# The attention output of batches 0 to 2 is turned by transfers and scaled by GpSimd

## The reference, cut to what matters

```python
def attention(Q, K, V, ...):                        # K = V = ctx
    q = _split_heads(Q @ Wq.T + bq)
    k = _split_heads(K @ Wk.T + bk)
    v = _split_heads(V @ Wv.T + bv)
    attn = softmax(einsum('bhqd,bhkd->bhqk', q, k) * scale)
    ctx = einsum('bhqk,bhkd->bhqd', attn, v)        # heads side by side: (B, S, 256)
    return ctx @ Wo.T + bo
x = x + tanh(g_xattn) * attention(layernorm(x), ctx, ctx, ...)
h = layernorm(x)
logits = h @ w_router                               # top 2 of 8, softmax over the two
moe    = sum over the two of score * ((silu(h @ fc1[e]) * gate) @ fc2[e])
shared = (silu(h @ gate_w) * (h @ up_w)) @ down_w
x = x + tanh(g_ffn) * (moe + shared)
```

## Time and profile before

| what | value |
|---|---|
| time, median of 3 runs | 473.4 us (473.13 to 475.3) |
| profiled execution | 472.9 us |
| its span | 471.2 us |
| PE busy | 461.7 us, 98% |
| DVE busy | 338.4 us, 72% |
| ACT busy | 255.7 us, 54% |
| POOL busy | 118.4 us, 25% |

### The profile page before, as it was taken

The page is one execution under the profiler, slowest core; times in us unless marked ns, Lnnn a source line. Parts: engine busy times, 40 slices in busy tenths (PEclk is TensorE's granted clock), DMA queues, the critical chain, the costliest instruction groups (busy, mean ns, idle before and its releaser), DMA issues.

```text
span 471.2 us, 8172 instructions
## 1 busy us (share of the span) xinstructions
PE 461.7 (98%) x2394; PEld 224.7 (48%) x2394; DVE 338.4 (72%) x858; ACT 255.7 (54%) x544; POOL 118.4 (25%) x143
## 2 busy tenths in 40 slices
PE   8999999999999999999999999999999999999997
PEld 8665422333333333333356564675555555555745
DVE  1888897888888888888847876665565656542574
ACT  1664476777777777777766212113676667631110
POOL 5594485000000000000001177640333223332000
PEclk9999999999999999999999999999999999999999
DMA  8668762956564555320000022232332223211931
GB/s 254 219 179 230 184 198 69 198 141 134 136 134 137 135 134 137 92 69 1 3 1 2 0 102 90 91 110 60 92 87 83 85 87 91 80 57 47 362 114 59
DMA packets 47532, 52.80 MB, mean 112 GB/s; under 512 B 8640, under 2 KB 39744, under 8 KB 47488
## 3 DMA queue, kind: packets, MB, share of 16 engines
q1 hardware_dynamic: 42688, 41.75, 33.1%
q0 software_dynamic: 3168, 8.69, 5.1%
q10 hardware_dynamic: 1632, 1.84, 1.2%
HBM read 34.52 MB, written 17.60 MB: 111 GB/s over the span
## 4 chain that ended last, share of the span: by engine, by line
PE 83%; DVE 6%; DMA 5%; SPq 3%; issue 1%; ACT 1%; POOL 1%; ACTq 0%; POOLq 0%; DVEq 0%
PE PS L1329 12%; PE PS L1241 11%; PE PS L1457 11%; PE PS L1504 10%; PE PS L1611 9%; PE PS L1517 6%; PE PS L1630 5%; PE PS L1606 3%; PE PS L1377 3%; PE PS L1292 3%; PE PS L1625 2%; PE PS L1339 2%; DMA X<-in_x_dram 2%; PE PS L1585 2%; PE PS L1593 2%; DMA q_parts<-R 1%
## 5 line engine op out<-in xcount | busy, mean ns | idle before, releaser
L782 DVE TENSOR_REDUCE nmax<-PS 128x1 f32<-128x512 f32 x256 | 161.8, 681 | 14.7 <-PE PS L1241 14.2
L664 ACT ACTIVATE R<-PS 128x512 f32<-128x512 f32 x256 | 133.2, 603 | 38.9 <-PE PS L1457 38.9
L1241 PE MATMUL PS<-R 96*128 96x512 bf16 x256 | 96.0, 381 | 0.7 <-DMA R<-k_parts 0.5
L1457 PE MATMUL PS<-R 98*128 98x512 bf16 x256 | 86.2, 379 | 1.8 <-DMA R<-mparts 1.5
L1329 PE MATMUL PS<-R 128*32 128x512 f32 x512 | 68.2, 605 | 0.0
L552 POOL DMA_INDIRECT token_y<-R,dest x34 | 32.8, 966 | 86.6 <-DVE R L1124 86.3
L1241 PEld LDWEIGHTS PS<-R 96*128 96x128 bf16 x256 | 24.8, 97 | 56.3 <-DVE nmax L782 39.4
L513 POOL TENSOR_TENSOR rstd<-var_eps,minus_half 128x4 f32<-128x4 f32 x4 | 4.1, 1024 | 187.7 <-DVE var_eps L765 187.7
L1611 PE MATMUL PS<-R 128*128 x100 | 47.3, 595 | 1.0 <-ACT R L738 1.0
L1457 PEld LDWEIGHTS PS<-R 98*128 98x128 bf16 x256 | 24.7, 97 | 41.1 <-ACT R L664 20.9
L683 ACT ACTIVATE R<-PS 128x512 f32<-128x512 f32 x16 | 9.6, 597 | 62.0 <-PE PS L1504 62.0
(11 more groups left out here) (173 smaller groups left out, 602.5 us busy)
## 6 DMA issues: line engine op xcount, KB each, us to landing
R<-q_parts SPq DMA_DIRECT2D x96, 64.0 KB, 3.1
R<-k_parts SPq DMA_DIRECT2D x96, 64.0 KB, 3.2
R<-in_fc_w_dram SPq DMA_DIRECT2D x16, 256.0 KB, 3.0
R<-token_y SPq DMA_DIRECT2D x4, 1024.0 KB, 10.2
R<-slot_x SPq DMA_DIRECT2D x25, 129.0 KB, 2.1
k_parts<-R SPq DMA_DIRECT2D x8, 384.0 KB, 3.2
q_parts<-R SPq DMA_DIRECT2D x8, 384.0 KB, 3.6
fc<-in_fc_w_dram SPq DMA_DIRECT2D x16, 128.0 KB, 3.0
```

Of the source, the lines that this page charges most:

```text
L664: nc.scalar.activation(PT[:, kt, j, :], PS[:, (G * (TB * i + kt) + j) % 3, :], ACT.Exp).then_inc(exp_done, 1)
L782: nc.vector.tensor_reduce(nmax[:, i % 2, j * TB + qt:j * TB + qt + 1], PS[:, smax_bank(n), :], AX.X, ALU.max, negate=True).then_inc(max_re ...
L1241: mm(PS[:, smax_bank(n), :], QS[g][0:KS, j, qt * P:(qt + 1) * P], KST[g][0:KS, j, :], start=True, stop=True).then_inc(smax_done, 1)
L1457: mm(PS[:, n % 3, :], KST[g][0:KM, j, kt * P:(kt + 1) * P], QS[g][0:KM, j, :], start=True, stop=True).then_inc(st_done, 1)
```

## The change

The context of the groups 0 to 11 (batches 0 to 2, `TURNED` = 12) keeps its features on partitions. SP stores the copy `OT` of a group to DRAM and sends the row of denominators of each head into `DENS`, 16 columns on 128 partitions. A group later SP reads the rows of features back, packed, as 64 partitions of `CTX` (which lies in the memory of `CH`); DVE takes the reciprocal in `DENS`' layout (`scale_of`), SP stores it, and another group later reads it back, repeated for the 16 features of each head, as 64 partitions of `SCALES` (the memory of the value weights). Once two groups are there, POOL multiplies 128x512 of `CTX` by `SCALES`. `out_projection` reads `CTX` in place. The transposes, `denominators` and `head_out` stay for batch 3.

With it: the experts' weights are loaded by POOL; the wait `parts_stored` moves from ahead of the loop into it; the tail's steps stand in another order; the column of token numbers in `CH` is written by POOL for each batch after its projection; `router_rows(3)` goes ahead of half a product; the last parts of the shared product of batch 1, their `shared_out` and the scales of the experts move into slots 0 to 2.

```diff
 @block.sync
+ def store_out(i):
+     sp.wait_ge(ot_ready, i + 1)
+     sp.dma_start(o_scr[i], OT[i % 2]).then_inc(o_out[i % 2], 16)
+     sp.dma_start(DENS[:, i % 2, :], OT[i % 2][DK:P:P // G, :].rearrange("j (q n) -> j q n", n=G * TB)).then_inc(den_in[i % 2], 16)
+ def load_out(i):
+     b, g = divmod(i, NG)
+     sp.wait_ge(o_out[i % 2], times(i))
+     sp.dma_start(CTX[64 * (g % 2):64 * (g % 2 + 1), b, g // 2, :],
+                  o_scr[i].rearrange("(j d) n -> j d n", j=G)[:, 0:DK, :]).then_inc(ctx_in[i // 2], 16)
+ def store_scale(i):
+     sp.wait_ge(scale_ready, i + 1)
+     sp.dma_start(r_scr[i].rearrange("j (q n) -> (j q) n", n=G * TB), SCALE[:, i % 2, :]).then_inc(scale_out[i % 2], 16)
+ def load_scale(i):
+     sp.wait_ge(scale_out[i % 2], times(i))
...
+     wait(sp, ctx_scaled, i // 2)
+     sp.dma_start(SCALES[64 * (i % 2):64 * (i % 2 + 1), :],
+                  r_scr[i].unsqueeze(1).to_broadcast([G, DK, S])).then_inc(ctx_in[i // 2], 16)
...
- for b in range(1, B):
-     parts_stored(b)
  for i in range(GROUPS):
+     if i and (i + 3) % NG == 0 and i + 3 < GROUPS:
+         parts_stored((i + 3) // NG)
      if 0 < i and i + 3 < GROUPS:
          load_group(i + 3)
      if i + 1 < GROUPS:
          load_max(i + 1)
...
-     if 2 <= i < 2 + E:
...                                   # 4 DMAs of fc1, fc2
+     if 0 <= i - 1 < TURNED:
+         store_out(i - 1)
+     if 0 <= i - 2 < TURNED:
+         load_out(i - 2)
+         store_scale(i - 2)
+     if 0 <= i - 3 < TURNED:
+         load_scale(i - 3)
 @block.gpsimd
  def rstd_second(b):
...
+     pool.wait_ge(wo_done, 2 * (b + 1))
+     nc.gpsimd.iota(CH[:, sl, D], ...).then_inc(tokens_in, 1)
+ def scale_context(n):
+     b, c = divmod(n, DC)
+     pool.wait_ge(ctx_in[n], 16 * 4)
+     nc.gpsimd.tensor_tensor(CTX[:, b, c, :], CTX[:, b, c, :], SCALES, ALU.mult).then_inc(ctx_scaled, 1)
...
+ for i in range(2, TURNED + 3):
+     if i < 2 + E:
+         pool.wait_ge(m2_ready, i + 2)
+         load_expert(i - 2)            # the 4 DMAs of fc1, fc2
+     if i >= 4 and i % 2 == 0:
+         scale_context((i - 4) // 2)
 @block.scalar
  def out_copy(i):
      act.wait_ge(pv_done, TB * (i + 1))
-     if i >= 2:
-         act.wait_ge(ot_t, i - 1)
+     if 2 <= i < TURNED + 2:
+         act.wait_ge(o_out[i % 2], times(i - 2))
+         act.wait_ge(den_in[i % 2], times(i - 2))
...
 @block.vector
+ def scale_of(i):
+     dve.wait_ge(den_in[i % 2], times(i))
...
+     nc.vector.reciprocal(SCALE[:, i % 2, :], DENS[:, i % 2, :]).then_inc(scale_ready, 1)
  def tail(n):
-     0: ctt_second(0)    1: residual(0), statistics(0)    2: ctt_second(1), normalised(0)
-     3: residual(1), statistics(1)    4: h2t_second(0), ctt_second(2), normalised(1)
-     5: logits_turned(0), logits(0), choose(0), residual(2), statistics(2)
+     0: residual(0), statistics(0)    2: normalised(0), residual(1), statistics(1)
+     3: h2t_second(0)    4: normalised(1), logits_turned(0), residual(2), logits(0)
+     5: statistics(2), choose(0)
  in the loop, behind the sixth maximum of group i:
+     if 0 <= i - 2 < TURNED:
+         scale_of(i - 2)
-     denominators(i - 1), head_out(i - 1) for every i
+     ... for i > TURNED
 @block.tensor
  def tail(n):
-     0: ctx_transpose(0)    1: out_projection(0)    2: ctx_transpose(1)    3: out_projection(1)
-     4: h2_transpose(0), ctx_transpose(2)
-     5: router(0), out_projection(2, (0,)), router_rows(0), out_projection(2, (1,))
+     0: out_projection(0)    1: out_projection(1, (0,))    2: out_projection(1, (1,))
+     3: h2_transpose(0), out_projection(2, (0,))
+     4: router(0), out_projection(2, (1,)), router_rows(0)
+     5: h2_transpose(1)
...
-         if kt == 1 and i:
+         if kt == 1 and i > TURNED:
              out_transpose(i - 1)
...
  values(GROUPS - 1, TB - 1)
- h2_transpose(1)
  rank(0)
...
- gate_up(1, 1)
+ gate_or_up(1, 1, 0)
  router_rows(3)
+ gate_or_up(1, 1, 1)
...
- down(BE - 1, 2)
+ down(BE - 1, TB)
  transpose_rows(0)
- down_part(BE - 1, IC - 1, 2)
- down_part(BE - 1, IC - 1, 3)
+ down_part(BE - 1, IC - 1, 0)
+ down_part(BE - 1, IC - 1, 1)      # parts 2 and 3 follow in slots 0 and 1
```

More of the change, by code:

```diff
@@ L304, in ctt, with times @@
         def ctt(b, c):
-            return CTT[:, b % 2, c, :]
+            return CTX[:, b, c, :] if b < B - 1 else CTT[:, c, :]
+        def times(i):
+            return 16 * (i // 2 + 1)
         @block.sync
@@ L1063, in _ @@
                             one_max(TB * s + qt)
-                        if i:
-                            n = TB * kt + qt - OUT_AT
-                            if n == 0:
-                                denominators(i - 1)
-                            elif n == 1:
-                                head_out(i - 1)
+                        n = TB * kt + qt - OUT_AT
+                        if n == 0 and 0 <= i - 2 < TURNED:
+                            scale_of(i - 2)
+                        if n == 0 and i > TURNED:
+                            denominators(i - 1)
+                        if n == 1 and i > TURNED:
+                            head_out(i - 1)
                         if TB * kt + qt == M2_AT and i + 1 < GROUPS:
@@ L1109, in _, with scales, slot_result @@
             tabulate_units()
-            for h in range(2):
-                shared_out(1, h)
-            dve.wait_ge(exp_sc, 1)
-            step(nc.vector.tensor_scalar(sc[:, 2, :], sc[:, 1, :], 1.0, None, ALU.add))
-            step(nc.vector.reciprocal(sc[:, 3, :], sc[:, 2, :]))
-            step(nc.vector.tensor_tensor(sc[:, 0, :], sc[:, 1, :], sc[:, 3, :], ALU.mult))
-            step(nc.vector.tensor_scalar(scg[:, 0, :], sc[:, 3, :], tg[:, 1:2], None, ALU.mult))
-            step(nc.vector.tensor_scalar(scg[:, 1, :], sc[:, 0, :], tg[:, 1:2], None, ALU.mult))
-            def slot_result(it, u):
-                dve.wait_ge(y_done, it * UN + u + 1)
-                wait(dve, y_out[u], it * 16)
+            def scales():
+                dve.wait_ge(exp_sc, 1)
+                step(nc.vector.tensor_scalar(sc[:, 2, :], sc[:, 1, :], 1.0, None, ALU.add))
+                step(nc.vector.reciprocal(sc[:, 3, :], sc[:, 2, :]))
+                step(nc.vector.tensor_tensor(sc[:, 0, :], sc[:, 1, :], sc[:, 3, :], ALU.mult))
+                step(nc.vector.tensor_scalar(scg[:, 0, :], sc[:, 3, :], tg[:, 1:2], None, ALU.mult))
+                step(nc.vector.tensor_scalar(scg[:, 1, :], sc[:, 0, :], tg[:, 1:2], None, ALU.mult))
+            def slot_result(j):
+                u = j % UN
+                dve.wait_ge(y_done, j + 1)
+                wait(dve, y_out[u], j // UN * 16)
                 nc.vector.tensor_copy(YE[:, u, :], PS[:, 5 + u, 0:D]).then_inc(y_ready, 1)
@@ L1164, in _ @@
                     destination(j + 1)
+                if j < 2:
+                    shared_out(1, j)
+                if j == 2:
+                    scales()
                 if j >= 2:
-                    slot_result(*divmod(j - 2, UN))
+                    slot_result(j - 2)
                 m, at = divmod(j - (FIRST_MIXED - UN), UN)
@@ L1349, in bank_free @@
                 if kind == "ctx_t":
-                    pe.wait_ge(ctt_ready[part], b + 1)
+                    pe.wait_ge(ctt_ready[part], 1)
                 if kind == "wo":
@@ L1370, in out_projection @@
                 pe.wait_ge(w_in["o"], 16)
-                for c in range(DC):
-                    pe.wait_ge(ctt_ready[c], b + 1)
+                if b < B - 1:
+                    pe.wait_ge(ctx_scaled, DC * (b + 1))
+                else:
+                    for c in range(DC):
+                        pe.wait_ge(ctt_ready[c], 1)
                 for h in halves:
```

121 lines of the change are left out of this document (64 added, 57 removed).

## The result

| | before | after |
|---|---|---|
| time, median of 4 runs | 473.8 us (473.13 to 475.3) | 486.8 us (484.85 to 487.32) |
| ratio to before, 95% interval | | 1.0262 [1.0236, 1.0288] |
| profiled execution, span | 472.9, 471.2 us | 486.76, 485.0 us |

The change makes the kernel 2.6% slower; 466.3 was forecast.

What follows compares the result with a forecast made beforehand. PE, busy 98% of the span, was taken as the bound. The terms -5.9 +2.0 -1.1 -1.9 -0.2 = -7.1 gave 465.8 us for the profiled execution, 466.3 against the median, range 463.0 to 469.6.

Steps and rivals of the forecast that it cites:

- Part 1: Attention loop: removing the transposes of twelve groups saves PE 0.49 us each, -5.9 us; steady group 11.47 us.
- Part 2: Steady groups: the packing's extra SP transfers and POOL's weight loads and scaling cost 0 us.
- 3.3 us of room: Steady groups: `mparts` lands at 204.3, the next group's first score product wants it at 207.64.
- rival A: Groups 3 to 14: shared DMA engines make `mparts` late and PE waits; 9.6 us on top, 475.9; chance 0.06.
- the rule on the slowest dimension: Packing transfers with slowest dimension 4 run on four DMA engines only; longer landings, sum not changed.
- Part 3: Group 2: first denominators land late, at 92.1, holding up DVE's maxima; PE waits +2.0 us (0.4 to 3.4).
- Part 4: Loop start: moving the `parts_stored` wait removes PE's wait for `mparts` at the second group, -1.1 us.
- Part 5: Last six key tiles: new order reaches the first shared product -1.9 us sooner, with a 2.0 us wait at `rank(0)`.
- Part 6: Behind the tail, up to slot 0: PE waits under 1 us for slot 0's rows; -0.2 us (-1.0 to +0.5).
- Rival D: Steady groups: DVE's queue, not PE, paces them, so no gain from the removed transposes; 472; chance 0.04.
- C: Group 2 and tail: the first denominators land before 89.5 and `choose(0)` doesn't delay PE; 462.3; chance 0.15.
- B: Early groups: denominators' transfer or POOL's weights hold up DVE in several, some 3 us more, 469.5; chance 0.17.

Runs made afterwards that it cites:

- e4: Kernel before, with two idle 4 KB transfers issued by SP between the two halves of `mparts` in groups 1 to 15: 490.46 us, ratio 1.0367.
- e12: The changed kernel again without any edit, on another chip: 483.14 us, 1.0158 of the kernel before.
- e9: Changed kernel with the dimensions of load_out and load_scale reordered, slowest 16 instead of 4, same bytes: 470.68 us, 0.9907 of the kernel before.
- e15: e9 plus three idle 4 KB transfers issued by SP behind the row of denominators in each of twelve groups: 483.11 us, 1.0195 of the kernel before.
- e1: Changed kernel without packing transfers and `scale_of`, `CTX` filled with ones, so the result is incomplete: 465.51 us, 0.9835 of the kernel before.
- e5: Changed kernel with all five packing transfers still issued but cut to tiny sizes, so the result is incomplete: 0.9812 of the kernel before.
- e8: Changed kernel with the packing transfers issued between the group loads and `mparts`, full computation: 0.994 of the kernel before.
- e3: Changed kernel with `mparts` of groups 1 to 15 issued by ACT on its own queue: 492.39 us, 1.0384 of the kernel before.
- e10: e9 with the row of denominators sent in four transfers, one per head: 485.42 us, 1.0214 of the kernel before.
- e6: Changed kernel with all packing transfers issued by POOL and the experts' weights back on SP: 0.9948 of the kernel before.

## Why the prediction failed, by its steps

**Part 1, right.** The group without waits is 11.50 us long, PE busy throughout, DVE 10.30, as forecast.

**Part 2 failed, and with it the sum.** "3.3 us of room" rests on the earlier trace rows, where I took the product at 207.64 for the first of the next group. Counting from the turned maxima (201.40) on, it is the second key tile's; the product that `mparts` releases is the one a key tile (2.8 us) after its issue. e4 points to it, since there PE's waits stand at this very place in the order of products. In the timeline of PE before it is

```profile
204.79 0.38 PE L1457 MATMUL PS<-R 98*128 98x512 bf16 x1
```

`mparts` lands at 202.6 + 1.7 = 204.3. The room is 0.5 us, and e4 measured 0.4 to 0.6. So rival A begins to cost once a landing comes 0.5 us later, not 3.3. The landings after have a median 0.6 above those before and a maximum 3.3 above: by the right room that is a wait in most groups, by mine in hardly any. Rival A was the right mechanism (landings late by the transfers that share the engines, paid in nine of the groups 4 to 14) with the wrong bar, and so I gave it 0.06 and a price of 9.6 us; the waits came to 16.1, and the 4.3 for PE's lower clock behind the two longest stood in no term. The second half of the error is that I let the rule on the slowest dimension "not change the sum": by e12 and e9 it was worth 12.5 us. The third is the sentence "Behind them on SP stand the group loads, which are wanted a group and a half later": true, but what counts is also what they are in the way of. In the change's own trace no `mparts` went out late for it, but three issues more on SP were enough (e15).

**Part 3, right in kind and within its range**: +2.0 on PE was forecast (0.4 to 3.4), and 1.13 came. DVE stood 1.90, since the row of denominators had landed by 91.6, not 92.1. DVE and PE after, in group 2:

```profile
91.59 0.25 DVE L904 RECIPROCAL SCALE<-DENS 128x16 f32<-128x16 f32 x1 [1.90 <-DMA DENS<-R]
```
```profile
92.44 0.39 PE L1300 MATMUL PS<-R 96*128 96x512 bf16 x1 [1.13 <-DVE nmax L837]
```

**Part 4, right**: no wait for `mparts` at group 1, which cost 1.08 before. **Part 5, right**: the stage is 2.07 shorter (1.9), with the wait at `rank(0)` 1.60 long (2.0) and ended by DVE's last step of `choose(0)`. PE after:

```profile
254.31 3.62 PE L1440 MATMUL PS<-w_o,CH 128*128 128x256 f32 x16
...
280.41 0.41 PE L1475 MATMUL PS<-OHS,before 128*128 128x32 f32 x2 [1.60 <-DVE PRE L1013]
...
281.35 1.88 PE L1565 MATMUL PS<-R,wgate 128*128 128x512 f32 x4
```

**Part 6, right in kind, too small in size**: -1.2 instead of -0.2 (-1.0 at the outside), still with a wait for the rows of slot 0:

```profile
332.65 0.41 PE L1647 MATMUL PS<-ident,R 128*128 128x128 f32 x2 [0.47 <-DMA R<-slot_x]
```

Rival D is refuted by part 1's window, C by the waits of parts 3 and 5, and B, in this execution, by part 3: one late row of denominators, not several. In e12, the same kernel again, there were two (5.2 us on DVE, 3.8 on PE with the maxima behind them), so that B isn't excluded. Without the packing the sum without part 3 is 464.3, and e1 measured 465.5: the step that failed was the transfer that all groups start with.

**Open**: why the change took 486.8 on one chip and 483.1 on another with the kernel before the same within 0.3 us; how the cost splits between load_out and load_scale, which were not tried apart; what the weights on POOL's queue do beside the packing, as in the longest waits; and why the chip of e5 to e8 needs 57.0 to 60.9 us for the stage of 51.3.

## What to carry to other kernels

Before adding transfers beside a small one that each round waits for, measure that one's room: find the very instruction that its semaphore releases, subtract issue and landing, and check it with an idle transfer put in front. Add up what the issuing engine issues in a round and compare it with the round: 9.9 us of 11.5 did no harm here, 12.1 did. Look at the order of dimensions also of transfers that nobody waits for soon: here 16 instead of 4 as the slowest, and nothing else in the loop, turned 1.6% slower into 0.9% faster.

## What the runs showed of the hardware

- Two idle 4 KB transfers, issued in 1.17 us, ahead of one small transfer cost 0.8 us in a steady group, and 3.7% of the kernel by the medians (e4).
- With three idle issues more a group, a round on SP took 12.1 us of a group of 11.5; `mparts` went out up to 2.3 us late and the kernel lost what it had gained (e15: 1.0195, e9: 0.9907).
- A small transfer alone in ACT's queue landed as late (median 2.6, maximum 10.3 us) as in SP's crowded one (e3); PE stood 0.5 us for ACT in 14 groups.
- The same 128 KB loads, in the order 4 x 16 rows or 16 x 4 rows of 2 KB, made 12.5 us of difference to the kernel and a median of 4.2 to 4.4 or of 3.2 us for the landing of other loads (e12, e9).
- After waits of 3.69 and 3.91 us PE's granted clock was 0.50 (the lower of its two levels, 1.2 of 2.4 GHz), for some 3 and 5 us; waits up to 1.97 us left it at 1.00 in the same execution. The length alone doesn't decide it: in e9 a wait of 1.97 us was followed by 3 us at 0.50, in e10 one of 1.55 was, and in e15 one of 2.52 was not. PE in e9:

```profile
108.99 0.60 PE L1523 MATMUL PS<-R 98*128 98x512 bf16 x2 [1.97 <-DMA R<-mparts]
...
109.65 0.62 PE L1523 MATMUL PS<-R 98*128 98x512 bf16 x1
```

- POOL issued the packing's transfers at 0.56 to 0.71 us each (e6), SP in the kernel after at medians of 0.45 to 0.61.
